# Splitting each half-tile key load into a 120-partition and an 8-partition transfer

## The reference, cut to what matters

```python
qe   = broadcast(q)                                   # [B, L, D]
feat = concat([qe, k, qe - k, qe * k], axis=-1)       # [B, L, 4D]
h    = feat @ W1 + b1                                 # [B, L, 64]
h    = where(h >= 0, h, alpha * h)
a    = (h @ W2 + b2)[..., 0]                          # [B, L]
a    = where(mask == 0, -1e9, a)
w    = softmax(a, axis=-1)
out  = einsum('bl,bld->bd', w, k)                     # [B, D]
```

## Time and profile before

| | us |
|---|---|
| median of three runs | 1024.97 |
| lowest and highest of them | 1015.89, 1025.12 |
| the profiled execution | 1018.95 |
| its span | 1017.0 |

### The profile page before, as it was taken

The page is one execution under the profiler, slowest core; times in us unless marked ns, Lnnn a source line. Parts: engine busy times, 40 slices in busy tenths (PEclk is TensorE's granted clock), DMA queues, the critical chain, the costliest instruction groups (busy, mean ns, idle before and its releaser), DMA issues.

```text
span 1017.0 us, 55327 instructions
## 1 busy us (share of the span) xinstructions
PE 847.9 (83%) x25216; PEld 559.4 (55%) x25216; DVE 769.4 (76%) x1143; ACT 532.8 (52%) x1281; POOL 656.3 (65%) x401
## 2 busy tenths in 40 slices
PE   0769888988888898889889889888887888888896
PEld 0435555655555565556555556555555555545564
DVE  2879777878788778787787888777886777867771
ACT  0355545655555565555555555555554555545552
POOL 0657666767667676676666667667666667657661
PEclk9899999999999999999998999999999999989999
DMA  8844766667776766786675777766677676667630
GB/s 253 322 148 138 268 204 212 233 201 239 253 236 228 238 206 230 238 270 211 229 231 185 236 266 238 232 223 226 204 242 257 211 230 209 217 225 233 213 103 11
DMA packets 67017, 222.45 MB, mean 219 GB/s; under 512 B 25312, under 2 KB 33504, under 8 KB 66784
## 3 DMA queue, kind: packets, MB, share of 16 engines
q1 hardware_dynamic: 66784, 218.92, 65.0%
HBM read 214.57 MB, written 4.33 MB: 215 GB/s over the span
## 4 chain that ended last, share of the span: by engine, by line
PE 40%; DVE 16%; DMA 15%; issue 13%; ACT 8%; SPq 7%; POOL 0%; DVEq 0%; ACTq 0%; POOLq 0%
PE hP L431 22%; DMA keys<-in_r_k 9%; PE poolP L472 9%; DVE act L348 9%; PE scoreP L460 7%; ACT act L289 6%; DVE keysT L340 5%; DMA probs_scratch<-expd 5%; SPq L160 3%; SPq L211 2%; ACT expd L313 2%; PE poolP L480 1%; DVE neg_max L361 1%; DVE logits L355 1%; DMA w2c<-in_L_rec_W 1%
## 5 line engine op out<-in xcount | busy, mean ns | idle before, releaser
L289 ACT ACTIVATE act<-hP,biast,al 128x200 f32<-128x200 f32 x1024 | 459.5, 515 | 329.6 <-PE hP L431 325.9
L340 DVE STREAM_TRANSPOSE keysT<-keys 128x768 f32<-128x768 f32 (+1 forms) x512 | 510.1, 997 | 60.4 <-DMA keys<-in_r_k 60.3
L431 PE MATMUL hP<-keysT,weff 32*64 32x200 f32 x16384 | 475.5, 344 | 30.3 <-issue 23.5
L232 POOL TENSOR_TENSOR weff<-qX,wp 128x1024 f32<-128x1024 f32 x128 | 244.0, 1906 | 324.3 <-PE hP L431 300.7
L431 PEld LDWEIGHTS hP<-keysT,weff 32*64 32x64 f32 x16384 | 310.2, 133 | 186.2 <-issue 113.1
L348 DVE TENSOR_TENSOR act<-hP,act 128x400 f32<-128x400 f32 x512 | 283.9, 554 | 146.8 <-ACT act L289 143.0
L236 POOL TENSOR_TENSOR weff<-weff,wk 128x1024 f32<-128x1024 f32 x128 | 303.2, 2369 | 10.0
L472 PE MATMUL poolP<-keys,pool_w 128*16 128x128 f32 x6400 | 244.6, 276 | 22.7 <-issue 21.2
L472 PEld LDWEIGHTS poolP<-keys,pool_w 128*16 128x16 f32 x6400 | 173.4, 97 | 98.1 <-issue 93.0
L460 PE MATMUL scoreP<-act,w2win 128*16 128x200 f32 x2048 | 151.3, 341 | 81.3 <-DVE act L348 70.3
L271 POOL TENSOR_TENSOR pool_w<-probs_k,own_b 128x400 f32<-128x400 f32 x128 | 111.3, 870 | 15.7 <-DMA probs_k<-probs_scratch 7.9
(11 more groups left out here) (35 smaller groups left out, 40.9 us busy)
## 6 DMA issues: line engine op xcount, KB each, us to landing
keys<-in_r_k SPq DMA_DIRECT2D x128, 832.0 KB, 5.5
keys<-in_r_k SPq DMA_DIRECT2D x128, 768.0 KB, 5.2
probs_scratch<-expd SPq DMA_DIRECT2D x32, 100.0 KB, 3.7
masks<-in_r_mask SPq DMA_DIRECT2D x128, 12.5 KB
probs_k<-probs_scratch SPq DMA_DIRECT2D x128, 12.5 KB
out_rows<-pooled SPq DMA_DIRECT2D x128, 8.0 KB
keys<-in_r_q SPq DMA_DIRECT2D x4, 256.0 KB, 5.0
act<-in_L_rec_W SPq DMA_DIRECT2D x4, 128.0 KB, 6.1
```

What stands on the lines that cost most here:

```text
L232: g_.tensor_tensor(weff[:, n % 2, :, :, :], qX[:, n, :, :].unsqueeze(3).broadcast_to([P, BQ, CD, H]), wp[:].unsqueeze(1).broadcast_to([P, ...
L289: a_.activation(act[:, k, a, :], hP[:, 2 * (p % HSETS) + a % 2, 0:L], ACT.Identity, bias=biast[:, n, k, a:a + 1], scale=al[:]).then_inc(t_ ...
L340: v_.transpose(keysT[:, n % TBUF, j0 * D:j1 * D], keys[:, n % SLOTS, j0 * D:j1 * D]).then_inc(keysT_done, 1)
L431: mm = t_.matmul(hP[H * r:H * r + H, 2 * (p % HSETS) + a % 2, 0:L], weff[QP * a:QP * a + QP, n % 2, w, c, :], kT[QP * a:QP * a + QP, :, c, ...
```

## The change

Each half of a tile is issued as two transfers, partitions 0 to 119 and partitions 120 to 127, one right after the other. Both raise the slot's semaphore by 16, so the two places that wait for a tile's keys wait for twice the count. Nothing else is changed: slots, cuts, the order of SP, and the other transfers are the same.

```diff
+SPREAD = 120
...
             def load_part(n, x):
                 at = slice(LOAD_CUT[x] * D, LOAD_CUT[x + 1] * D)
-                sp.dma_start(keys[:, n % SLOTS, at], k_tiles[n][:, at]).then_inc(keys_in[n % SLOTS], 16)
+                for rows in (slice(0, SPREAD), slice(SPREAD, P)):
+                    sp.dma_start(keys[rows, n % SLOTS, at], k_tiles[n][rows, at]).then_inc(keys_in[n % SLOTS], 16)
...
                 if n > 2:
-                    sp.wait_ge(keys_in[n - 2], 16 * LOADS)
+                    sp.wait_ge(keys_in[n - 2], 16 * 2 * LOADS)
...
                 if piece == 0:
-                    dve.wait_ge(keys_in[n % SLOTS], (n // SLOTS + 1) * 16 * LOADS)
+                    dve.wait_ge(keys_in[n % SLOTS], (n // SLOTS + 1) * 16 * 2 * LOADS)
```

## The result

The changed kernel is slower: 1240.95 us median (1235.57 to 1249.69, four runs) against 1020.43 us for the kernel before on the same chip, a ratio of 1.225 with a 95% interval of 1.219 to 1.231. The forecast was 993 us in a range of 968 to 1050. The profiled execution took 1249.69 us with a span of 1247.6.

A forecast was written before the change was run, and what follows sets the result against it. PE was taken to set the pace, its idle time partly instruction fetches held up behind keys. Fetches -39, groups +6 and start +1 gave -32 us from 1025: 993 us, range 968 to 1050.

The forecast's parts named there:

- Issue time on SP: SP's 256 added key transfers: covered by waits per tile, but 0.7 us a group (0.33 to 1.23) in the group's chain.
- The ninth row: Eight DMA engines carry nine rows of a half instead of eight: 0.34 us a row, 0.5 us a group (0.3 to 1.0).
- Fetches: PE's instruction fetches find the freed DMA engine without keys: 39 us gained of 56.5 us of "issue" gaps (bounds 0 to 56.5).
- the first rival: Fetches not on the freed engine, or gaps not fetches: only costs are left, 1052 us (1035 to 1075), chance 0.23.
- as before: Sign of a wrong prediction: PE's "issue" waits unchanged from 56.5 us, with DVE's key waits rising towards 90 us.
- Sum over the groups: Net cost in the once-a-group key chain over 29 waits: +6 us with the right engine freed, +35 us if not.
- The third: Rival: 120 rows go over eight engines, a half takes 2.4 us more, keys become the bound: above 1200 us, chance 0.02.
- q8's packets: Sign in the instruction-fetch queue: if the prediction is right, its packets still number about 198.
- the issue waits: Sign on PE: waits with releaser "issue" fall from 56.5 us to under 15 if right, stay as they were if wrong.
- DVE's waits for keys: Sign on DVE: if the prediction is wrong, these rise from 60.3 us towards 90.
- SP's waits for DVE: Sign on SP: its 394.9 us of waits for DVE's transposes fall by 256 times the issue price.

The follow-up runs named there:

- e4: The changed kernel with each half-tile as 88 + 40 partitions in place of 120 + 8: 1263 us, ratio 1.241 to the kernel before.
- e10: The changed kernel with each half-tile as 104 + 24 partitions in place of 120 + 8: 1254 us in one run.
- e7: The changed kernel with 120 + 8 for each tile's first half only, the second half one 128-partition transfer: 1163 us, ratio 1.144 to the kernel before.
- e5: The kernel before with each half-tile as three transfers, partitions 32 to 95, 0 to 31, 96 to 127: 1142 us, ratio 1.123.

## Why the prediction was wrong

**The step that failed** is the one that stood under "Issue time on SP" and "The ninth row": a 120-partition transfer was priced as a 128-partition one plus 0 to 0.3 us of issue. The time of its rows was not a term at all. The median 6,656-byte row went from 253 to 453 ns in the kernel, and alone a transfer took 5.93 against 4.44 us. No row that I had read of the kernel before shows it, as no transfer of more than a few bytes there goes to 64 or 120 partitions; but the range should have had a bound for it. And the packet records of the kernel before held a hint: its queries come in 32 partitions a transfer, and their 2,048-byte rows took a median of 153 ns, where the rate of a 253 ns key row makes 78 ns (an estimate). I looked up which engines a 120-row transfer uses, and not into which partitions each then writes. The Trainium skill's page SBUF — State Buffer, Door 1: The DMA port swizzle, has the map of the ports. Counting ports by it would have warned of 64 + 64, whose halves reach 8 of 16 ports each, but not of 120 partitions, which reach all 16. What the count leaves out is which engines write one port at the same time.

**Fetches.** The mechanism was right: PE's "issue" gaps are fetches held up behind key rows. The table at e4 shows it fetch by fetch, with 4.0 us of gaps behind the four places whose engine is free and 58.9 us behind the four others, and e10 bears it out. The place was wrong: they go round eight engines, and the freed one is not among them. So the 39 us were 0, which the first rival said. And what became of the gaps was worse than "as before": a fetch stands behind rows that take 1.4 times as long in the mean, and 56.5 us grew to 156.2.

**Sum over the groups.** Priced at +6 to +35 us. The issues themselves were at the low end (0.30 us for 8 partitions, 0.45 to 0.47 for 120). The ninth row's 0.34 us was worked out from 1.7 us for "a transfer of hardly any data", but L208 moves 100 KB, so that reading was wrong; and the price of the slower rows came on top. In the two groups shown, the chain's last load went from 4.44 to 7.21 us; the weights' way out took 5.5 us in the median for 3.7; and PE's waits before the scores grew by 49.6 us over the run.

**PE's clock** was no term either. Its mean granted share over 100 to 950 us was 0.99 before and 0.91 over 100 to 1170 us after, 1.0 being 2.4 GHz and 0.5 being 1.2 GHz: the lower level for some 18% of the time. Over the whole run the lower level held for 232 us after and for 37 before. The windows of PE of both kernels, before first (us, busy, clock, DMA share, GB/s):

```profile
100.00:950.00 850.00, 737.07 (x22058) 0.99 0.69 228
```
```profile
100.00:1170.00 1070.00, 816.60 (x22379) 0.91 0.79 184
```

The same first-layer matmuls (L431 before, L433 after) had a median of 328 ns in both and a mean of 368 for 344. In every kernel here whose PE idled more, the granted clock was lower: 0.88 to 0.93 in the split ones, 0.97 to 0.99 in those with 128 partitions. In the changed kernel PE stood idle for 59% of the 5 us ahead of a fall of the clock, in the mean of the 46 falls after the start, and for 24% of the time overall; so the falls come behind idle stretches. No run changes PE's gaps alone, so that they lower the clock is argued and not shown by itself.

**The rivals.** The first (fetches elsewhere, 1052 us) had the right half of the cause and lacked the other. The third, with a chance of 0.02, had the right time and a half that takes over 2 us longer (2.8 us in the group's chain shown, 1.5 us alone). Its cause is refuted: 120 rows went over fifteen engines (15 in flight). Nor did the keys simply become the bound: on PE the waits before the scores are 49.6 us of the loss, the "issue" gaps 99.7 and the busy time 77.6. That its time came out right is luck. Of the signs, q8's packets stayed at 198, and the issue waits and DVE's waits for keys both rose, the latter far past the 90 us given. One sign failed: SP's waits for DVE were to fall by 256 times the issue price, and they rose from 394.9 to 444.0 us (L193 223.9, L154 220.1).

## What to carry to other kernels

Price a reshaped transfer by its rows' time, not only by its issues and its count of engines: work out which partitions each engine writes and whether two engines meet in one write port. Where a row of the trace can't show it, one transfer by itself, waited for, does. In the queue that issues everything, look at what stands between the event and the load that an engine waits for: two reorderings of SP's program, found in the same rows, gave 4.2% (ratio 0.958, interval 0.953 to 0.963), while each alone gave 1 to 2%.

## What the runs showed that I had not expected

- The fetches of PE's instructions go round eight engines in a fixed order, one every 5 to 6.3 us, and leave alone the one that 120 partitions do not use.
- The same 64 source rows take 4.36 us into partitions 0 to 63 and 3.60 us into 32 to 95.
- A transfer over 128 partitions is slower when it stands behind one of 120 + 8: mean row 361 ns in e7, against 309 before.
- e5's "issue" gaps were only 49.6 us although its rows took 377 ns on average. Why the fetches cost less there is open.
